# A wait on TensorE's progress ahead of every fourth gather of router rows

## What is computed

```python
h = (x_flat @ W_gat).reshape(M, HEADS, NUM_EXPERTS)
a_src = (h * att_src).sum(-1); a_dst = (h * att_dst).sum(-1)
e = leaky_relu(a_src[src] + a_dst[dst], negative_slope=0.2)
e_max = segment_max(e, dst); ee = exp(e - e_max[dst])
denom = segment_sum(ee, dst)
agg = segment_sum(h[src] * ee / denom[dst], dst) + b_gat
scores = layernorm(agg, ...).reshape(M, HEADS, NUM_EXPERTS).mean(1)
w = softmax(top_k(scores, 2))
for ei in range(NUM_EXPERTS):
    hh = gelu(x @ W1[ei] + b1[ei])
    out = out + g[..., None] * (hh @ W2[ei] + b2[ei])
```

## Times and profile before

| | us |
|---|---|
| time, median of 3 runs | 4270.76 |
| lowest and highest run | 4270.12 and 4277.53 |
| span of the profiled execution | 5331.2 |
| graph stage in the profile, up to the first router gather | 2833.2 |
| expert stage in the profile, up to TensorE's last matmul | 2133.7 |
| final stage in the profile | 364.3 |

### The profile page before, as it was taken

One profiled execution on the slowest core, in us unless ns is written; L12 is line 12 of the kernel. 1 busy time (PEld: TensorE's weight loads), 2 busy tenths in 40 slices (PEclk: granted clock), 3 DMA queues, 4 the chain that ended last, 5 costly groups with the idle time before them and its releaser, 6 DMA issues. The chain is left out here.

```text
span 5331.2 us, 46344 instructions
## 1 busy us (share of the span) xinstructions
PE 3564.3 (67%) x12937; PEld 2313.0 (43%) x12938; DVE 2082.9 (39%) x4892; ACT 801.1 (15%) x1970; POOL 2832.6 (53%) x2937
## 2 busy tenths in 40 slices
PE   0688888888757777777626377768685777789200
PEld 0455555555445455555413154444453454455100
DVE  5456655665546555544311020211111120212378
ACT  5111211111101111111101011111111111112000
POOL 2666666666666666666655623653636444630420
PEclk9889899998878888888767588888787788899655
DMA  7444444444445555555512111211112111211387
GB/s 250 128 109 115 112 111 112 112 115 112 112 111 148 138 153 154 162 152 152 125 33 61 18 49 28 58 38 48 35 50 43 44 48 36 60 50 48 118 254 253
DMA packets 381413, 540.57 MB, mean 101 GB/s; under 512 B 120314, under 2 KB 297818, under 8 KB 381143
## 3 DMA queue, kind: packets, MB, share of 16 engines
q0 software_dynamic: 119136, 234.44, 20.0%
q1 hardware_dynamic: 243119, 288.12, 16.8%
q10 hardware_dynamic: 19016, 16.48, 0.9%
HBM read 392.03 MB, written 146.74 MB: 101 GB/s over the span
## 5 line engine op out<-in xcount | busy, mean ns | idle before, releaser
L788 POOL DMA_INDIRECT rows<-xn_rows,gsrc x1664 | 1606.6, 965 | 908.5 <-issue 459.8
L1357 POOL DMA_INDIRECT nb<-route_rows,idx x1024 | 1000.3, 977 | 897.7 <-DVE msg L1432 480.9
L1093 PE MATMUL PS<-rows,oh 128*128 128x257 f32 x3328 | 910.0, 427 | 351.9 <-issue 220.0
L1686 PE MATMUL PS<-arena,hid 128*125 128x256 f32 x3200 | 865.1, 422 | 408.5 <-issue 298.6
L1686 PEld LDWEIGHTS PS<-arena,hid 128*125 128x125 f32 x3200 | 662.9, 209 | 621.3 <-issue 502.6
L1093 PEld LDWEIGHTS PS<-rows,oh 128*128 128x128 f32 x3328 | 693.8, 214 | 488.8 <-issue 296.6
L1621 DVE TENSOR_TENSOR y_sb<-PS,b_b 125x512 f32<-125x512 f32 x200 | 128.7, 685 | 1781.4 <-remote 975.2
L1678 PE MATMUL PS<-x2g,arena 128*128 128x500 f32 x1600 | 722.6, 610 | 147.3 <-issue 94.0
L1678 PEld LDWEIGHTS PS<-x2g,arena 128*128 128x128 f32 x1600 | 313.5, 197 | 541.6 <-issue 473.0
L1647 ACT ACTIVATE hid<-PS,b_sb 128x500 f32<-128x500 f32 x400 | 269.9, 677 | 1109.9 <-PE PS L1678 688.9
L1165 PE MATMUL PS<-own_w,p_t 128*125 128x512 f32 x400 | 231.2, 662 | 77.7 <-ACT s_t L1053 54.5
(11 more groups left out here) (304 smaller groups left out, 3086.8 us busy)
## 6 DMA issues: line engine op xcount, KB each, us to landing
y_rows<-y_sb SPq DMA_DIRECT2D x100, 512.0 KB
arena<-y_rows SPq DMA_DIRECT2D x100, 512.0 KB
rows<-xn_rows,gsrc POOLq DMA_INDIRECT x1664
nb<-route_rows,idx POOLq DMA_INDIRECT x1024
sum_rows<-kept SPq DMA_DIRECT2D x104, 128.5 KB
x_rows<-x SPq DMA_DIRECT2D x100, 128.0 KB
hid<-x_rows SPq DMA_DIRECT2D x100, 128.0 KB
m_in<-sum_rows SPq DMA_DIRECT2D x100, 125.5 KB
```

The lines of the kernel that those rows point to most:

```text
L788: pool.indirect_dma_start(out=rows[w][h][:, q, 0:D], out_offset=None, in_=xn_rows, in_offset=bass.IndirectOffsetOnAxis(ap=gsrc[:, s * HU + ...
L1093: last = mm(SUM[:, 0:D + 1], oh[w][h][:, q, :], rows[w][h][:, q, :], start=h == 0 and q == 0, stop=h == 1 and q == HU - 1)
L1357: pool.indirect_dma_start(out=nb[b % NBUF][:, c, :], out_offset=None, in_=route_rows, in_offset=bass.IndirectOffsetOnAxis(ap=idx[:, b * W ...
L1686: last = mm(Y[j % 2][e // 2][0:NP, (e % 2) * D:(e % 2 + 1) * D], hid[:, 4 * e + k, j * NP:(j + 1) * NP], w2_sb[:, e, k, :], start=k == 0, ...
```

## The change

Ahead of every fourth gather of a batch GpSimd gets one more wait, on a constant value of one of TensorE's two counters. The value stands for a place in the experts' tiles: gather c of batch b goes with tile (b + c/64) x 5.65 + 1. The new function `where_pe_is` turns a place into a counter and a count: within the first half of a group of four tiles it is `s_hp`, eight chunks for a tile; within the second half it is `s_y`, two tiles' outputs for each tile of the place. No other instruction changes; 5.65 only gets a name.

```diff
+SPREAD = 4
+TILES_A_BATCH = 5.65
...
-    t = int((b + 1) * 5.65) + 3
+    t = int((b + 1) * TILES_A_BATCH) + 3
     return t if t % 4 < 2 else t + 4 - t % 4
+
+def where_pe_is(tiles):
+
+    group, rest = int(tiles // 4), tiles % 4
+    if rest < 2:
+        return 0, group * 16 + int(rest * 8) + 1
+    return 1, group * 4 + int((rest - 2) * 2)
...
                     if b >= NBUF:
                         pool.wait_ge(s_nbf, b - NBUF + 1)
                     for c in range(W):
+                        if c % SPREAD == 0:
+                            at = (b + c / W) * TILES_A_BATCH + 1
+                            which, count = where_pe_is(at)
+                            pool.wait_ge((s_hp, s_y)[which], count)
                         if (b or c) and c % REST == 0:
```

## The result

The changed kernel takes **4296.98 us** (median of 4 runs, 4290.94 to 4298.83). The ratio is 1.0056, with an interval of 1.0041 to 1.007, which is 18 to 30 us. The medians lie 26.5 us apart: the change makes the kernel slower, as forecast, and by nearly as much as forecast (4294 us, 23 more than before).

What follows compares the result with a forecast made beforehand. GpSimd's path was taken to bound the expert stage: 2401 + (1484 + 23) + 364 = 4272 us against 4249 before, so the median goes from 4270.8 to 4294 us; the range of 8 in 10 is 4263 to 4306.

Steps and rivals of the forecast that it cites:

- GpSimd bounds the stage: Expert stage, timed runs: GpSimd's path of 1484 us, not TensorE's 1410 us, sets the length.
- The first wait is the price: Ahead of batch 0's first gather: 26.9 us of head start lost, all later gathers 23.4 us late.
- The other 255 waits and the instructions are free: Expert stage: GpSimd falls some 9 us a batch behind, so no later wait holds; 256 satisfied waits taken as 0 us.
- The terms of the sum: Whole kernel before: graph stage 2401, expert stage 1484 and final stage 364 us, together 4249 us.
- long gathers: Beside the scans of `records`: one gather a batch may take 3.34 instead of 0.94 us, 38 us more on GpSimd's path.
- The profile of the changed kernel: Profile after: span 5331 give or take 60 us, waits on TensorE replacing 480.9 us on buffers, groups of 80 to 90 us.
- "Sum": Step adding up the stages: profile span hardly changed at 5331 us, timed median from 4270.8 to 4294 us.
- The slow matmuls are real: Rival, expert stage: slow groups also occur in timed runs and spreading gathers cures them; 4223 us, chance 0.08.

Runs made afterwards that it cites:

- disturbed recording: First profile of the unchanged kernel before: span 5331.2 us, against 4270.8 us timed.
- A shorter GpSimd path: Kernel before with one full landing wait in 64 gathers in place of one in 16: 4166.1 us (0.9752).
- 336 us more of TensorE's work: Kernel before with the first 8 of 16 chunks of each group computed twice: 4468.05 us (1.0465).
- `REST` 64 and 2048: Kernel before with `REST`, gathers per full landing wait, raised from 16; both values make the same program: 4166.1 and 4169.12 us.
- the two pairs with a shorter GpSimd path: Kernel before and changed kernel, both with fewer full landing waits: 4166.1 and 4190.83 us; repeated, 4169.12 and 4192.05 us.
- From batch 4 on: Changed kernel without the new waits of batches 0 to 3, the other 192 kept: 4271.29 us (0.9998 to the kernel before).
- as instructions: Changed kernel with all 256 waits on a count that `s_fe` has long reached, so none holds: 4273.08 us (1.0004 to the kernel before).
- second profile of before: Kernel before, unchanged, profiled once more: span 4263.2 us.

## Why the prediction was right, and where it was not

- **GpSimd bounds the stage: right.** The rows of a disturbed recording named TensorE; the sum of the stages against the median named GpSimd. A shorter GpSimd path gives 107.5 us, 336 us more of TensorE's work cost 199.6, and the change costs nothing once TensorE's path is the longer one.
- **The first wait is the price: right, in its working too.** Alone it costs 22.8 us of the 26.5, and without the early waits nothing is lost. The term was 23.4 us: 26.9 of head start, less 3.5 because the first 18 gathers run slowly at the start of the stage (26.66 us for 17 pitches) and not so slowly later (23.2). This was read from a disturbed recording, but it holds in the undisturbed ones: GpSimd's idle time is 26.87 us, the 17 pitches take 27.28 us before and 23.13 after, and the 18th gather comes 23.8 us late. From there on the lateness wanders with the landing waits, between 21.7 and 29.9 us, and is 28.9 at the last gather. These last 5 us are not shown to be the change's: two recordings of one program (`REST` 64 and 2048) differ by 7.7 us from the 18th gather to the last. The price was 26.5 us between the medians here, and 22.8, 24.7 and 22.9 us in the first wait alone and the two pairs with a shorter GpSimd path.
- **The other 255 waits and the instructions are free: right, within a few us.** From batch 4 on: 4271.29; as instructions: 4273.08. The 63 other waits of batches 0 to 3 were not run alone; the whole change costs 3.7 us more than the first wait alone, and the intervals of the two overlap.
- **The terms of the sum: right in total, off one by one.** The second profile of before has 2384.1 us up to the first gather (predicted 2401), 1547.1 from there to TensorE's end (1484, or 1522 with long gathers) and 332.0 after it (364). The stage was under-sized in its gathers, not in its tail: first to last 1465.5 us against 1400 or 1438, and then 81.6 us against 84. Longer gathers were real: the 1024 take 1012.1 us by the page, 45 more than at the usual 0.944, against an estimate of 38. The gaps ahead of the 63 landing waits average 2.37 us instead of 2.22, some 10 us more, and other gaps give as much again. The two outer stages, read from the disturbed recording, were over-sized by 49 us together. That these errors nearly cancel is luck: 4249 and 4287 enclose the median, but no stage in them has the length that was measured.
- **The profile of the changed kernel: wrong.** A span of 5331, give or take 60, was expected, with waits on TensorE instead of the 480.9 us and groups of 80 to 90 us; the span is 4294.1 and the groups take 55.5. The failed step is the one that opens "Sum". It took the slow-down for a thing of every recording of this program, when the rows showed one recording only. No time in the forecast rested on that step, but the signs named for it (no groups of 55.5 us among the first twenty, waits on TensorE about as long as the 480.9 us) did not come: 16 groups of 25 take 55.5 us, and 53.4 us of waits are put down to TensorE.
- **The slow matmuls are real: wrong as a rival.** They are not in the second profile of the same program.

## What to carry to other kernels

Ahead of pacing an engine by another's progress, ask which of the two is late over the stage: where the paced engine is the late one, every wait but the first is already met, and the first is paid at the end (here 23 to 27 us for some 27 us of idleness). Where a profile is far longer than the timed runs, add up the pitches of each engine from it and hold the sums against the timed median, stage by stage; the sums named the right engine here although the waits in the trace named the other. And look at the waits inside the bounding engine's own loop first: leaving out three of four waits for landings gave four times what the change lost.

## What the hardware showed that was not expected

- One recording of a program can be a quarter longer than another of the same program: 5331.2 and 4263.2 us, with GpSimd's busy time nearly the same (2832.6 and 2849.9) and TensorE's longer by 343 us, and gaps of up to some 2.2 us ahead of single matmuls. The bytes on each DMA queue are the same in both, those of the two instruction queues among them (0.74 and 0.79 MB).
- One gather is held up in nearly every `records`. In the changed kernel gathers run beside the scans of 15 of the 16 `records`, and in each of the 15 one gather takes 2.55 to 4.12 us instead of 0.94, 13 of them above 3.3. One of them, from the timeline:

```profile
3720.34 5.32 DVE L1450 TENSOR_TENSOR_SCAN rec<-dd,rec,msg 128x64 f32<-128x64 f32 x20
...
3720.96 1.07 POOL L1371 DMA_INDIRECT nb<-route_rows,idx  x1 [0.30 <-issue]
3722.34 4.12 POOL L1371 DMA_INDIRECT nb<-route_rows,idx  x1 [0.30 <-issue]
```

The scans end at 3725.66. Of the two gathers beside them the first takes 0.13 us more than usual, and the second is not done until 0.80 us behind the scans. In all 15, and in the 15 of the second profile of before, the held gather ends 0.79 to 0.80 us behind the last scan, whenever it began, while those that begin ahead of it beside the same scans take 0.94 to 1.08 us. The Trainium skill, SBUF — State Buffer, section Who interferes with whom, says that a VectorE instruction with two inputs from SBUF contends with a GpSimd instruction that reads SBUF, and that the pair of ports which they share is locked exclusively. The trace agrees for the held gather and not plainly for those ahead of it; and the held one waits through as many as 13 of the 20 scans, each an instruction of its own of 0.27 us. What decides between them was not tried.
